# A Flamingo block on one core: rows of the wide expert blocks turned by SBUF-to-SBUF DMAs and VectorE in place of TensorE

## The chip, the cores and the metric

The kernel runs on one core of a Trainium2 chip. The metric is the device time of one execution in microseconds (us), the median of the runs. The engines are TensorE (PE; PEld is its weight load), VectorE (DVE), ScalarE (ACT), GpSimd (POOL) and SyncE (SP), which only issues DMAs here. Each works through its own queue of instructions in program order; semaphores tie them together.

## The reference

The input is x of 4 x 1024 rows of 256 numbers. It computes

```
x = x + tanh(g_xattn) * cross_attention(layernorm(x), ctx)     # 16 heads, 77 context rows
x = x + tanh(g_ffn) * ffn(layernorm(x))
ffn(x) = silu(x sg^T) * (x su^T) sd^T                          # shared expert, 688 wide
       + sum over 4 experts e: comb[e] * (silu(x eg[e]^T) * (x eu[e]^T)) ed[e]^T
```

where comb holds the weights of the two best experts of each row and zero for the others. All is fp32; the kernel splits a matmul operand into a high and a low fp32r part and makes three products (high*high, high*low, low*high).

## The kernel before

The first 450 us hold the attention, the shared expert, the routing table and the preparation of the experts' weights. The 4096 rows are normalised once and stored in DRAM (xn_scratch). After routing, the 8192 pairs of row and expert, sorted by expert, are worked off in 13 wide blocks of 512 rows (NB = 13, BT = 4 tiles of 128 rows) and then 15 narrow tiles of 128 rows (small_tiles). The change is in the wide blocks (big_tiles) and in the first narrow tile.

For wide block j:

- GpSimd gathers the 512 rows with four indirect DMAs (L501) into big_xin, and adds the four result tiles into the output with four more (L509). Its queue runs: gather j+2, additions of block j, gather j+3, and so on. A gather waits until big_xin is free.
- TensorE transposes big_xin in eight 128x128 squares (x_T, L605) into two PSUM banks, p_m and p_t. This is done at chunk 3 of block j-1.
- ScalarE copies them as the high part, big_fxT_hi (x_hi, L522), and VectorE subtracts that from PSUM and writes the low part, big_fxT_lo (x_lo, L554).
- The hidden width of 688 is worked in six chunks (FC = 6, chunk 5 being short). For each chunk c TensorE computes gate and up (gate_up, L623, 12 matmuls of 512 columns), ScalarE takes the silu (L537), VectorE the product (inner, L569), ScalarE its high part (h_hi, L542), VectorE the low part (h_lo, L576 and L579), and TensorE multiplies chunk c-2 by the down weights (down, L640). ScalarE (weights_hi, L529) and VectorE (weights_lo, L562) copy out the expert's weights three chunks ahead.
- At chunk 1 VectorE scales the four result tiles of block j-1 (result, L586) from the two banks p_f.

The order on each engine is written out by hand. At chunk 3 ScalarE runs silu, weights_hi, h_hi, then the two x_hi of block j+1; VectorE runs inner, h_lo, weights_lo, then the two x_lo. Gate/up of chunk 0 of block j+1 waits for both x_lo:

```
            if c == 0:
                pe.wait_ge(s_xlo, rows_done(j))
```

At the seam between the wide blocks and the narrow tiles, VectorE's step of tile 0 multiplies, scales the last four result tiles (last_results), and then makes the low part of tile 1's rows (x_lo in small_tiles, L274), for which TensorE's gate/up of tile 1 (L341) waits. SP has no work in the wide blocks; its last is storing the shared expert's results. Block 0's rows are turned while the preparation of the experts' weights ends: TensorE's last preparation transposes (of raw and tail) come after gate/up of chunk 1 of block 0.

Of the kernel before, what the change touches and what calls it, by code (L numbers as in the profile page):

```python
# [5 lines left out]
f32r = mybir.dt.float32r  # L6
# [6 lines left out]
P = 128  # L13
# [16 lines left out]
E = 4  # L30
# [25 lines left out]
CUT = FF - P // 2  # L56

# [91 lines left out]
def small_tiles(nc, v, sem, place, banks, s_add):  # L149
# [129 lines left out]
    def on_vector(dve, last_results):  # L279
# [159 lines left out]
def big_tiles(nc, v, m, place, banks):  # L439
# [6 lines left out]
    (s_rows, s_xT, s_xhi, s_xlo, s_whi, s_wlo, s_gu, s_sil, s_hid, s_hhi, s_hlo, s_last, s_y, s_yo, s_add,  # L446
     s_turn) = (m[k] for k in (
         "s_rows s_xT s_xhi s_xlo s_whi s_wlo s_gu s_sil s_hid s_hhi s_hlo s_last s_y s_yo s_add s_turn").split())
# [4 lines left out]
    fxT.append([sb(f"big_fxT1_{s}", [P, KC, WIDE], f32r) for s in ("hi", "lo")])  # L453
# [40 lines left out]

    def on_gpsimd(pool):
        def gather(j):
            if j > 0:
                pool.wait_ge(s_xT, rows_done(j - 1))
# [15 lines left out]
    def on_scalar(act):  # L514
# [31 lines left out]
    def on_vector(dve):  # L546
# [4 lines left out]

        def x_lo(j, c):
            dve.wait_ge(s_xhi, rows_done(j, c))
            nc.vector.tensor_tensor(fxT[j % 2][1][:, c, :], p_x[c][:, :], fxT[j % 2][0][:, c, :],  # L554
                                    ALU.subtract).then_inc(s_xlo, 1)
# [35 lines left out]
        return hold, x_lo, weights_lo, inner, h_lo, result  # L591

    def on_tensor(pe):
# [5 lines left out]
        def x_T(j):  # L599
            pe.wait_ge(s_rows, 16 * BT * (j + 1))  # L600
            if j > 0:
                pe.wait_ge(s_xlo, rows_done(j - 1))
# [5 lines left out]
        def gate_up(j, c):  # L608
# [8 lines left out]
            for half in range(2 if c < FC - 1 else 1):  # L617
                for k in range(KC):
                    for q, (w, x) in enumerate(PASSES):
# [3 lines left out]
                        last = nc.tensor.matmul(p_gu[c % 2][half][0:out_rows, :], lhsT, fxT[j % 2][x][:, k, :],  # L623
# [23 lines left out]
        return hold, x_T, gate_up, down  # L647

    return {"gpsimd": on_gpsimd, "scalar": on_scalar, "vector": on_vector, "tensor": on_tensor}


def attend_share_route(nc, v):
# [8 lines left out]
    with st:  # L661
# [159 lines left out]
        s_add, s_rows = sem("s_add"), sem("s_rows")  # L821
# [3 lines left out]
        big = big_tiles(nc, v, {"s_rows": s_rows, "s_xT": s_xnT, "s_xhi": s_xnhi, "s_xlo": s_xnlo, "s_whi": s_whi,  # L825
# [104 lines left out]
        def _(sp):  # L930
# [1020 lines left out]
        def _(dve):  # L1951
# [650 lines left out]
            hold, x_lo, weights_lo, big_inner, big_h_lo, big_result = big["vector"](dve)  # L2602
# [13 lines left out]
            def big_step(j, c):  # L2616
# [26 lines left out]
            def last_results():  # L2643
                for t in range(BT):
                    big_result(NB - 1, t)
# [4 lines left out]
        def _(pe):  # L2650
# [567 lines left out]
            hold, big_x_T, big_gate_up, big_down = big["tensor"](pe)  # L3218
            big_x_T(0)
# [3 lines left out]
            def big_step(j, c):  # L3223
# [65 lines left out]
```

## Time and profile before

| | |
|---|---|
| median of 3 runs | 884.07 us (882.83 to 884.09) |
| the profiled execution | 881.68 us, its span 879.9 us |
| TensorE busy | 846.5 us, 96% |
| VectorE busy | 581.9 us, 66% |
| ScalarE busy | 520.8 us, 59% |
| GpSimd busy | 461.2 us, 52% |
| wide blocks | from about 453 us to about 769 us |
| DMA | 62.05 MB in 56887 packets |

The span goes from the first to the last instruction; busy is the time in which an engine had an instruction under way. TensorE's matmuls are pipelined, so that one starts before the last has ended: its price is the distance between starts, not the duration shown. A share over the whole span says nothing of a stage.

### The profile page before, as it was taken

How to read it: one execution, taken by the hardware profiler on the slowest of the kernel's cores; microseconds unless marked ns; L12 is line 12 of the kernel's file. 1: busy time of each engine (PE TensorE's matmuls, PEld its weight loads, DVE VectorE, ACT ScalarE, POOL GpSimd, SP SyncE). 2: the span in 40 equal slices, each digit the busy share in tenths (PEclk: the TensorE clock that was granted, in tenths of full speed). 3: DMA queues.
4: the chain of work that ended last, by engine and by line, in shares of the span. 5: the costliest groups of instructions: out<-in, count | busy, mean ns of one | idle time of the engine just before them, and what ended most of it. 6: DMA issues, size and time to landing. Idle time of an engine off the chain costs nothing.

```text
span 879.9 us, 19161 instructions
## 1 busy us (share of the span) xinstructions
PE 846.5 (96%) x6271; PEld 742.7 (84%) x6272; DVE 581.9 (66%) x1203; ACT 520.8 (59%) x1846; POOL 461.2 (52%) x551
## 2 busy tenths in 40 slices
PE   8788999999999999999999999999999999999995
PEld 7566788888888799999988888888888888889994
DVE  6899899999998577876564555555555545444442
ACT  4999999999999444656464444444445444322221
POOL 6686767667565353676531454444443444364442
PEclk9899999999999999999999999999999999999998
DMA  7125233322313222333240333222222232232221
GB/s 219 42 77 180 68 90 94 90 66 90 90 66 96 73 74 85 120 103 103 86 141 25 49 49 49 43 41 38 41 41 42 47 48 37 31 49 42 36 40 20
DMA packets 56887, 62.05 MB, mean 71 GB/s; under 512 B 15642, under 2 KB 45183, under 8 KB 56799
## 3 DMA queue, kind: packets, MB, share of 16 engines
q1 hardware_dynamic: 42871, 43.15, 15.8%
q0 software_dynamic: 12864, 17.57, 12.7%
q8 instruction: 48, 0.79, 0.4%
q14 instruction: 40, 0.33, 0.1%
q10 hardware_dynamic: 1064, 0.21, 0.1%
HBM read 34.78 MB, written 25.82 MB: 69 GB/s over the span
## 4 chain that ended last, share of the span: by engine, by line
PE 85%; ACT 5%; DVE 5%; issue 2%; DMA 1%; POOL 1%; DVEq 0%; SPq 0%; ACTq 0%; POOLq 0%
PE p_s L623 23%; PE p_f L640 12%; PE p_f L2767 9%; PE p_s L341 6%; PE p_f L2812 5%; PE p_s L2767 4%; ACT prob L1484 4%; PE p_t L2698 3%; PE p_t L352 3%; PE p_s L2684 3%; PE p_m L2725 3%; PE p_m L2665 2%; PE p_m L2713 2%; PE p_s L2812 2%; PE p_s L2870 1%
## 5 line engine op out<-in xcount | busy, mean ns | idle before, releaser
L509 POOL DMA_INDIRECT out_rows<-big_yout,slot_id x52 | 86.6, 1666 | 158.2 <-DVE big_yout L586 146.3
L1484 ACT ACTIVATE prob<-p_s,negmax 128x77 f32<-128x77 f32 x512 | 161.1, 372 | 7.2 <-DVE negmax L2032 7.0
L537 ACT ACTIVATE big_sil<-p_s 128x512 f32<-128x512 f32 (+1 forms) x78 | 46.6, 597 | 144.7 <-PE p_s L623 126.1
L1484 ACT ACTIVATION_READ_ACCUMULATOR prob<-p_s,negmax 128x1 f32 x512 | 128.9, 255 | 0.0
L569 DVE TENSOR_TENSOR big_hid<-p_s,big_sil 128x512 f32<-128x512 f32 (+1 forms) x78 | 54.0, 692 | 99.5 <-ACT big_sil L537 88.5
L623 PE MATMUL p_s<-big_fxT_hi,big_w_hi 128*128 128x512 f32 (+1 forms) x286 | 113.8, 398 | 0.3 <-ACT big_w_hi L529 0.3
L623 PE MATMUL p_s<-big_fxT_lo,big_w_hi 128*128 128x512 f32 (+1 forms) x286 | 112.7, 394 | 0.0
L623 PE MATMUL p_s<-big_fxT_hi,big_w_lo 128*128 128x512 f32 (+1 forms) x286 | 112.2, 392 | 0.0
L1108 POOL TENSOR_TENSOR prob<-prob,rinv 128x616 f32<-128x616 f32 x64 | 78.5, 1236 | 62.1 <-DVE rinv L2039 62.1
L1127 POOL TENSOR_TENSOR shT_lo<-shid,shT_hi 128x256 fp32r<-128x256 f32 x80 | 63.0, 800 | 44.4 <-ACT shT_hi L1526 44.3
L640 PE MATMUL p_f<-wd_hi,big_hT_hi 128*128 (+1 forms) x312 | 85.5, 280 | 0.0
L640 PE MATMUL p_f<-wd_lo,big_hT_hi 128*128 (+1 forms) x312 | 85.3, 279 | 0.0
L2767 PE MATMUL p_f<-xnT_hi,swgu_hi 128*128 128x256 f32 x248 | 75.5, 304 | 0.8 <-DVE shid L2055 0.8
L640 PE MATMUL p_f<-wd_hi,big_hT_lo 128*128 x260 | 72.7, 279 | 0.0
L2767 PE MATMUL p_f<-xnT_hi,swgu_lo 128*128 128x256 f32 x248 | 69.6, 281 | 0.0
L2767 PE MATMUL p_f<-xnT_lo,swgu_hi 128*128 128x256 f32 x248 | 69.5, 280 | 0.0
L576 DVE TENSOR_TENSOR big_hT_lo<-big_hid,big_hT_hi 128x512 fp32r<-128x512 f32 (+1 forms) x65 | 44.9, 690 | 35.6 <-ACT big_hT_hi L542 28.6
L501 POOL DMA_INDIRECT big_xin<-xn_scratch,slot_id x52 | 51.4, 989 | 31.9 <-issue 17.2
L623 PEld LDWEIGHTS p_s<-big_fxT_hi,big_w_lo 128*128 128x128 f32 (+1 forms) x286 | 53.0, 185 | 13.1
L542 ACT ACTIVATE big_hT_hi<-big_hid 128x512 fp32r<-128x512 f32 (+1 forms) x78 | 49.3, 632 | 23.1 <-DVE big_hid L569 21.4
L623 PEld LDWEIGHTS p_s<-big_fxT_hi,big_w_hi 128*128 128x128 f32 (+1 forms) x286 | 53.0, 185 | 10.3 <-DVE big_fxT_lo L554 0.5
L640 PEld LDWEIGHTS p_f<-wd_hi,big_hT_hi 128*128 128x128 f32 (+1 forms) x312 | 58.6, 188 | 3.5
(341 smaller groups left out, 2537.7 us busy)
## 6 DMA issues: line engine op xcount, KB each, us to landing
xr<-in_x SPq DMA_DIRECT2D x16, 256.0 KB, 2.9
x_scratch<-xr SPq DMA_DIRECT2D x16, 256.0 KB, 2.8
xn_scratch<-xn SPq DMA_DIRECT2D x16, 256.0 KB, 2.1
xt_scratch<-xnT SPq DMA_DIRECT2D x16, 256.0 KB, 3.2
xin<-xt_scratch SPq DMA_DIRECT2D x16, 256.0 KB, 3.6
x1in<-x_scratch SPq DMA_DIRECT2D x16, 256.0 KB, 3.3
out_rows<-syout SPq DMA_DIRECT2D x16, 256.0 KB, 2.2
raw<-in_L_ffn_ed SPq DMA_DIRECT2D x4, 688.0 KB, 4.3
```

The lines of the kernel that those rows point to most:

```text
L341: last = nc.tensor.matmul(p_gu[:, g0:g1], fxT[a][:, c, :], wgu[b][:, bass.ds(e * KC + c, 1), g0:g1], start=(c == 0 and q == 0), stop=(c == ...
L501: pool.indirect_dma_start(xin[:, t, :], None, v["xn_d"], bass.IndirectOffsetOnAxis(slot_id[:, column(j, t)], 0)).then_inc(s_rows, 16)
L509: pool.indirect_dma_start(out, bass.IndirectOffsetOnAxis(slot_id[:, column(j, t)], 0), yout[:, t, :], None, compute_op=ALU.add).then_inc(s ...
L542: act.activation(hT[n % 3][0][0:r, :], hid[n % 2][0:r, :], ACT.Copy).then_inc(s_hhi, 1)
L569: nc.vector.tensor_tensor(hid[n % 2][0:r, :], up, sil[n % 2][0:r, :], ALU.mult).then_inc(s_hid, 1)
L623: last = nc.tensor.matmul(p_gu[c % 2][half][0:out_rows, :], lhsT, fxT[j % 2][x][:, k, :], start=(k == 0 and q == 0), stop=(k == KC - 1 and ...
L640: last = nc.tensor.matmul(p_y[t // 2][:, t % 2 * H:(t % 2 + 1) * H], hT[n % 3][h][0:r, at], wd[w][0:r, bass.ds(e * FC + c, 1), :], start=( ...
L1108: pool.tensor_tensor(pr_, pr_, rinv[:, t, m * HH:(m + 1) * HH].unsqueeze(2).broadcast_to([P, HH, SK]), ALU.mult).then_inc(s_P, 1)
L1127: pool.tensor_tensor(hT[1][:, c, :], hid[:, c, :], hT[0][:, c, :], ALU.subtract).then_inc(s_hlo, 1)
L1484: last = act.activation(prob[n % 2][t][:, m * PW + h * SK:m * PW + (h + 1) * SK], p_s[:, 2 * t + h // 4, col:col + SK], ACT.Exp, bias=negm ...
L2767: last = nc.tensor.matmul(bank[:, j * UT * P:(j + 1) * UT * P], swgu[w][:, k, j * SGU + c * P:j * SGU + (c + 1) * P], xns[x][:, n % 2, k, ...
L2812: nc.tensor.matmul(bank[:, t * H:(t + 1) * H], hT[x][:, c, at], swd[w][:, c, :], start=(c == 0 and q == 0), stop=False)
```

## The change

For blocks 1 to 12 TensorE no longer transposes. When the gathered rows have landed, SP issues 16 DMAs that place the sixteen 32x32 block positions of every 128x128 square transposed as blocks (rows 32b to 32b+31, columns 32a to 32a+31 go to partitions 32a and on, columns 32b and on) in a new tile, big_placed. VectorE then turns each 32x32 block in place (flip, two instructions of 128x512), into big_turned, which lies over the low part's memory. x_hi and x_lo read it instead of PSUM. The flips stand at chunk 3 of the block before, where x_lo stood, and the two x_lo move to chunk 4. SP's placing waits for the rows, for the flip of the block before and, for the first, for the end of the preparation. GpSimd's gathers wait for the placing instead of the transposes. fxT is laid out by tile and then by half, so that gate/up reads it in four runs of 128 columns. Block 0 is still transposed by TensorE.

At the seam the first narrow tile now takes two of the last four results, then x_lo of tile 1, then the other two.

```diff
@@ small_tiles, on_vector, step @@
-            if isinstance(j, int) and j == 0:
-                last_results()
+            first = isinstance(j, int) and j == 0
+            if first:
+                last_results(0)
             if not last:
                 x_lo(j + 1)
+            if first:
+                last_results(1)
@@ big_tiles @@
-    fxT = [[sb(f"big_fxT0_{s}", [P, KC, WIDE], f32r) for s in ("hi", "lo")]]
+    fxT = [[sb(f"big_fxT0_{s}", [P, BT, KC, P], f32r) for s in ("hi", "lo")]]
...
+    placed = sb("big_placed", [P, BT * KC, P])
...
+    def all_placed(j):
+        return 16 * SIDES * SIDES * j
+
+    def on_sync(sp):
+        def place(j):
+            sp.wait_ge(s_rows, 16 * BT * (j + 1))
+            if j > 1:
+                sp.wait_ge(s_flip, 2 * (j - 1))
+            rows = xin[:, :, :].rearrange("p t (k i) -> p (t k) i", k=KC)
+            for a in range(SIDES):
+                for b in range(SIDES):
+                    sp.dma_start(placed[a * TURN:(a + 1) * TURN, :, b * TURN:(b + 1) * TURN],
+                                 rows[b * TURN:(b + 1) * TURN, :, a * TURN:(a + 1) * TURN]).then_inc(s_placed, 16)
...
         def gather(j):
-            if j > 0:
-                pool.wait_ge(s_xT, rows_done(j - 1))
+            if j == 1:
+                pool.wait_ge(s_xT, rows_done(0))
+            elif j > 1:
+                pool.wait_ge(s_placed, all_placed(j - 1))
@@ on_scalar, x_hi, for j > 0 @@
-            act.wait_ge(s_xT, rows_done(j, c))
-            act.activation(fxT[j % 2][0][:, c, :], p_x[c][:, :], ACT.Copy).then_inc(s_xhi, 1)
+                act.wait_ge(s_flip, 2 * (j - 1) + c + 1)
+                act.activation(fxT[j % 2][0][:, pair, :, :].rearrange("p t k i -> p (t k i)"),
+                               turned[j % 2][:, pair, :, :].rearrange("p t k i -> p (t k i)"),
+                               ACT.Copy).then_inc(s_xhi, 1)
@@ on_vector @@
+        def flip(j, c):
+            dve.wait_ge(s_placed, all_placed(j))
+            if j > 1:
+                dve.wait_ge(s_gu, chunks_done(FC * (j - 1)))
+            blocks = slice(2 * KC * c, 2 * KC * (c + 1))
+            pair = slice(2 * c, 2 * c + 2)
+            nc.vector.transpose(turned[j % 2][:, pair, :, :].rearrange("p t k i -> p (t k i)"),
+                                placed[:, blocks, :].rearrange("p n i -> p (n i)")).then_inc(s_flip, 1)
@@ on_tensor, gate_up @@
-  lhsT, fxT[j % 2][x][:, k, :],
+  lhsT, fxT[j % 2][x][:, :, k, :],
@@ the queue of SP, behind the last store_y @@
+            place = big["sync"](sp)
+            sp.wait_ge(s_etr, PER * E)
+            sp.wait_ge(s_tail, 2 * E + 2)
+            for j in range(1, NB):
+                place(j)
@@ the queue of VectorE, big_step @@
-                        x_lo(j + 1, 0)
-                        x_lo(j + 1, 1)
+                        flip(j + 1, 0)
+                        flip(j + 1, 1)
+                if c == 4 and not last:
+                    x_lo(j + 1, 0)
+                    x_lo(j + 1, 1)
@@ the queue of TensorE, big_step @@
-                if c == 3:
-                    if j < NB - 1:
-                        big_x_T(j + 1)
-                    else:
-                        pe.wait_ge(s_xnlo, NU + KC * NB)
-                        small_x_T(0, 0)
+                if c == 3 and j == NB - 1:
+                    pe.wait_ge(s_xnlo, NU + KC * NB)
+                    small_x_T(0, 0)
```

## Rows read from the trace of the kernel before

**Rows 1.** The page: TensorE in 40 slices, in tenths, and its granted clock.

```profile
PE   8788999999999999999999999999999999999995
PEclk9899999999999999999999999999999999999998
```

**Rows 2.** Timeline of TensorE in block 8: start us, us, engine, line, operation, operands.

```profile
660.99 0.60 PE L605 MATMUL p_m<-ident,big_xin 128*128 128x128 f32 x4
...
661.78 0.47 PE L623 MATMUL p_s<-big_fxT_hi,big_w_hi 128*112 128x512 f32 x1
...
668.81 0.40 PE L623 MATMUL p_s<-big_fxT_hi,big_w_hi 128*128 128x512 f32 x1
```

**Rows 3.** Timeline of ScalarE in block 8; in brackets its idle time and releaser.

```profile
659.78 0.60 ACT L537 ACTIVATE big_sil<-p_s 128x512 f32<-128x512 f32 x1 [2.21 <-PE p_s L623]
...
661.14 0.63 ACT L542 ACTIVATE big_hT_hi<-big_hid 128x512 fp32r<-128x512 f32 x1 [0.24 <-DVE big_hid L569]
661.68 0.58 ACT L522 ACTIVATE big_fxT_hi<-p_m 128x512 fp32r<-128x512 f32 x1
...
664.81 0.60 ACT L537 ACTIVATE big_sil<-p_s 112x512 f32<-112x512 f32 x1 [2.07 <-issue]
```

**Rows 4.** Timeline of VectorE in block 8.

```profile
660.41 0.69 DVE L569 TENSOR_TENSOR big_hid<-p_s,big_sil 128x512 f32<-128x512 f32 x1 [1.91 <-ACT big_sil L537]
661.80 0.69 DVE L576 TENSOR_TENSOR big_hT_lo<-big_hid,big_hT_hi 128x512 fp32r<-128x512 f32 x1 [0.70 <-ACT big_hT_hi L542]
662.41 0.42 DVE L562 CAST big_w_lo<-wgu_lo 128x512 fp32r x1
662.75 0.68 DVE L554 TENSOR_TENSOR big_fxT_lo<-p_m,big_fxT_hi 128x512 fp32r<-128x512 f32 x1
...
665.44 0.69 DVE L569 TENSOR_TENSOR big_hid<-p_s,big_sil 112x512 f32<-112x512 f32 x1 [1.41 <-ACT big_sil L537]
666.83 0.69 DVE L576 TENSOR_TENSOR big_hT_lo<-big_hid,big_hT_hi 112x512 fp32r<-112x512 f32 x1 [0.70 <-issue]
667.44 0.48 DVE L562 CAST big_w_lo<-wgu_lo 128x512 fp32r x1
```

**Rows 5.** Timeline of GpSimd from block 8 into block 9.

```profile
654.82 2.00 POOL L509 DMA_INDIRECT out_rows<-big_yout,slot_id  x1 [11.30 <-DVE big_yout L586]
...
662.86 1.01 POOL L501 DMA_INDIRECT big_xin<-xn_scratch,slot_id  x1 [0.44 <-issue]
...
666.72 0.95 POOL L501 DMA_INDIRECT big_xin<-xn_scratch,slot_id  x1 [0.30 <-issue]
678.93 2.00 POOL L509 DMA_INDIRECT out_rows<-big_yout,slot_id  x1 [11.26 <-DVE big_yout L586]
```

**Rows 6.** Timelines of block 0: TensorE, GpSimd and VectorE, a row of each.

```profile
459.72 0.38 PE L2867 MATMUL p_m<-ident,tail 128*128 128x128 f32 x2
...
455.42 0.95 POOL L501 DMA_INDIRECT big_xin<-xn_scratch,slot_id  x1 [0.30 <-issue]
...
470.11 0.68 DVE L554 TENSOR_TENSOR big_fxT_lo<-p_m,big_fxT_hi 128x512 fp32r<-128x512 f32 x1
```

**Rows 7.** SP's copies by line (ns min/median/max), and the page's DMA queue and issue.

```profile
L952 SPq DMA_DIRECT2D vblk<-vall x96: 544/744/1162, 19.0 to 240.9; - x96
...
L146 SPq DMA_DIRECT2D raw<-in_L_ffn_eu x4: 521/523/523, 81.3 to 441.1; - x4
...
q1 hardware_dynamic: 42871, 43.15, 15.8%
...
xn_scratch<-xn SPq DMA_DIRECT2D x16, 256.0 KB, 2.1
```

**Rows 8.** Timelines at the seam: VectorE, then TensorE.

```profile
771.00 1.65 DVE L586 TENSOR_SCALAR big_yout<-p_f,slots 128x256 f32<-128x256 f32 x4
772.57 0.41 DVE L274 TENSOR_TENSOR fxT_lo<-p_m,fxT_hi 128x256 fp32r<-128x256 f32 x1
...
773.14 0.90 PE L341 MATMUL p_s<-wgu_hi,fxT_hi 128*128 x3 [0.78 <-DVE fxT_lo L274]
```

More of the change, by code:

```diff
@@ L56 @@
 CUT = FF - P // 2
+TURN = 32
+SIDES = P // TURN
 PASSES = ((0, 0), (0, 1), (1, 0))
@@ L445, in big_tiles @@
     p_x, p_gu, p_y = banks
-    (s_rows, s_xT, s_xhi, s_xlo, s_whi, s_wlo, s_gu, s_sil, s_hid, s_hhi, s_hlo, s_last, s_y, s_yo, s_add,
-     s_turn) = (m[k] for k in (
-         "s_rows s_xT s_xhi s_xlo s_whi s_wlo s_gu s_sil s_hid s_hhi s_hlo s_last s_y s_yo s_add s_turn").split())
+    (s_rows, s_xT, s_placed, s_flip, s_xhi, s_xlo, s_whi, s_wlo, s_gu, s_sil, s_hid, s_hhi, s_hlo, s_last, s_y, s_yo,
+     s_add, s_turn) = (m[k] for k in (
+         "s_rows s_xT s_placed s_flip s_xhi s_xlo s_whi s_wlo s_gu s_sil s_hid s_hhi s_hlo s_last s_y s_yo s_add "
+         "s_turn").split())
     sb = Home(nc, *place["ring"]).sb
     xin = sb("big_xin", [P, BT, H])
-    fxT = [[sb(f"big_fxT0_{s}", [P, KC, WIDE], f32r) for s in ("hi", "lo")]]
+    fxT = [[sb(f"big_fxT0_{s}", [P, BT, KC, P], f32r) for s in ("hi", "lo")]]
     sb = Home(nc, *place["raw"]).sb
-    fxT.append([sb(f"big_fxT1_{s}", [P, KC, WIDE], f32r) for s in ("hi", "lo")])
+    fxT.append([sb(f"big_fxT1_{s}", [P, BT, KC, P], f32r) for s in ("hi", "lo")])
+    placed = sb("big_placed", [P, BT * KC, P])
+    turned = []
+    for k, home in enumerate(("ring", "raw")):
+        sb = Home(nc, *place[home]).sb
+        if home == "ring":
+            sb("big_xin_again", [P, BT, H])
+        sb(f"big_fxT{k}_hi_again", [P, BT, KC, P], f32r)
+        turned.append(sb(f"big_turned{k}", [P, BT, KC, P]))
     sb = Home(nc, *place["th"]).sb
@@ L520, in x_hi @@
         def x_hi(j, c):
-            act.wait_ge(s_xT, rows_done(j, c))
-            act.activation(fxT[j % 2][0][:, c, :], p_x[c][:, :], ACT.Copy).then_inc(s_xhi, 1)
+            pair = slice(2 * c, 2 * c + 2)
+            if j == 0:
+                act.wait_ge(s_xT, rows_done(j, c))
+                act.activation(fxT[0][0][:, :, c, :], p_x[c][:, :].rearrange("p (t i) -> p t i", t=BT),
+                               ACT.Copy).then_inc(s_xhi, 1)
+            else:
+                act.wait_ge(s_flip, 2 * (j - 1) + c + 1)
+                act.activation(fxT[j % 2][0][:, pair, :, :].rearrange("p t k i -> p (t k i)"),
+                               turned[j % 2][:, pair, :, :].rearrange("p t k i -> p (t k i)"),
+                               ACT.Copy).then_inc(s_xhi, 1)
         def weights_hi(n):
@@ L550, in hold @@
             dve.reg_load(held[j % 2], expert_of[0:1, j:j + 1])
+        def flip(j, c):
[3 more added lines that the diff above has]
+            blocks = slice(2 * KC * c, 2 * KC * (c + 1))
+            pair = slice(2 * c, 2 * c + 2)
+            nc.vector.transpose(turned[j % 2][:, pair, :, :].rearrange("p t k i -> p (t k i)"),
+                                placed[:, blocks, :].rearrange("p n i -> p (n i)")).then_inc(s_flip, 1)
         def x_lo(j, c):
             dve.wait_ge(s_xhi, rows_done(j, c))
-            nc.vector.tensor_tensor(fxT[j % 2][1][:, c, :], p_x[c][:, :], fxT[j % 2][0][:, c, :],
-                                    ALU.subtract).then_inc(s_xlo, 1)
+            if j == 0:
+                nc.vector.tensor_tensor(fxT[0][1][:, :, c, :], p_x[c][:, :].rearrange("p (t i) -> p t i", t=BT),
+                                        fxT[0][0][:, :, c, :], ALU.subtract).then_inc(s_xlo, 1)
+            else:
+                low, whole, high = (x[:, 2 * c:2 * c + 2, :, :].rearrange("p t k i -> p (t k i)")
+                                    for x in (fxT[j % 2][1], turned[j % 2], fxT[j % 2][0]))
+                nc.vector.tensor_tensor(low, whole, high, ALU.subtract).then_inc(s_xlo, 1)
         def weights_lo(n):
@@ L589, in result @@
                 last.then_inc(s_yo, 1)
-        return hold, x_lo, weights_lo, inner, h_lo, result
+        return hold, flip, x_lo, weights_lo, inner, h_lo, result
     def on_tensor(pe):
@@ L597, in hold, with first_x_T @@
             pe.reg_load(held[j % 2], expert_of[0:1, j:j + 1])
[L599 to L602, printed above, removed]
+        def first_x_T():
+            pe.wait_ge(s_rows, 16 * BT)
             for c in range(KC):
@@ L622, in gate_up @@
                         out_rows = r if c < FC - 1 else 2 * r
-                        last = nc.tensor.matmul(p_gu[c % 2][half][0:out_rows, :], lhsT, fxT[j % 2][x][:, k, :],
+                        last = nc.tensor.matmul(p_gu[c % 2][half][0:out_rows, :], lhsT, fxT[j % 2][x][:, :, k, :],
                                                 start=(k == 0 and q == 0), stop=(k == KC - 1 and q == 2))
@@ L645, in down @@
                     last.then_inc(s_y, 1)
-        return hold, x_T, gate_up, down
-    return {"gpsimd": on_gpsimd, "scalar": on_scalar, "vector": on_vector, "tensor": on_tensor}
+        return hold, first_x_T, gate_up, down
+    return {"sync": on_sync, "gpsimd": on_gpsimd, "scalar": on_scalar, "vector": on_vector, "tensor": on_tensor}
 def attend_share_route(nc, v):
@@ L820, in attend_share_route @@
             "s_spread", "s_row", "s_til", "s_val", "s_vid", "s_vlo", "s_table"))
-        s_add, s_rows = sem("s_add"), sem("s_rows")
+        s_add, s_rows, s_placed, s_flip = (sem(n) for n in ("s_add", "s_rows", "s_placed", "s_flip"))
         late = small_tiles(nc, v, sem, {"ring": ring, "x1in": (x1in_home, xns_home), "raw": (raw_home, tail_home),
@@ L2601, in _ @@
                 e_lo(G)
-            hold, x_lo, weights_lo, big_inner, big_h_lo, big_result = big["vector"](dve)
+            hold, flip, x_lo, weights_lo, big_inner, big_h_lo, big_result = big["vector"](dve)
             hold(0)
@@ L2641, in _, with last_results @@
                     big_step(j, c)
-            def last_results():
-                for t in range(BT):
-                    big_result(NB - 1, t)
+            def last_results(pair):
+                for t in range(2):
+                    big_result(NB - 1, 2 * pair + t)
             late["vector"](dve, last_results)
```

7 lines of the change are left out of this document (4 added, 3 removed).

## The prediction

> **What bounds the kernel now.** I read the page first, for the slices: over the thirteen wide blocks TensorE's slices stand at 9 and its granted clock too, and neither falls until the last slice [rows 1]. So in the blocks TensorE sets the pace, and time taken off it is gained as long as nothing else is late. To see what would be late next I read the timelines of one block (block 8) engine by engine. TensorE runs gate/up of chunk 3, a share of the down product, then eight transposes of the next block's rows (the row shows the first four) from 660.99 to 661.78, then gate/up of chunk 4, and it enters block 9 at 668.81 without a pause [rows 2]. ScalarE and VectorE idle between short bursts and seem to have room [rows 3, 4]; but each is a queue in program order, and inside a chunk they alternate (silu, product, high part, low part), so what counts is the length of that chain and not their busy share. GpSimd's queue shows the period: the first addition of results is issued at 654.82 and again at 678.93, so a block takes 24.11 us [rows 5].
>
> **What is removed.** Eight transposes per block, 0.79 us of TensorE by the difference of starts (661.78 - 660.99) [rows 2]. Twelve of the thirteen blocks lose them: 12 x 0.79 = 9.5 us, if TensorE stays the bound. The page "TensorE: Matmul & The Clock Gate" of the Trainium skill (Part 4) gives about 275 ns for such a transpose in a kernel, so eight would be 2.2 us and twelve blocks 26 us by it; the trace's starts, about 0.1 us apart, are against that reading, and I keep 0.79.
>
> **What is added on the chain.** This is the step that decides. Before, x_hi and x_lo of the next block read PSUM as soon as TensorE had transposed, and the two subtracts were over about 1.3 us after 662.75, before the silu of chunk 4 at 664.81 [rows 3, 4]. Now at chunk 3 VectorE does flip, flip in the place of x_lo, x_lo; ScalarE's two x_hi wait for the flips, and ScalarE's silu of chunk 4 stands behind them; VectorE's x_lo, x_lo come only after the low part and the weights of chunk 4, and the next block's first gate/up waits for the second. I lay that chain out on block 8's clock, with F the duration of a flip and f the distance to the start of the next instruction:
> Silu of chunk 3 starts at 659.78, the first flip where the first x_lo stood, at 662.75 [rows 3, 4]. The second flip starts at 662.75 + f and ends at 662.75 + f + F. The second x_hi starts 0.04 later, as the high part does behind the product (660.41 + 0.69, then 661.14). It reads SBUF now, so I give it the high part's distance to the next start, 0.54 (661.68 - 661.14): silu of chunk 4 starts at 663.33 + f + F. From silu to product is 0.63 (665.44 - 664.81), to the low part 1.39 (666.83 - 665.44), to the weights 0.61 (667.44 - 666.83), to the first x_lo 0.34 (662.75 - 662.41), to the second x_lo 0.61 (a subtract that reads two SBUF tiles, as 661.80 to 662.41), its duration 0.69, and 0.16 until TensorE's matmul starts, as at the seam (772.57 + 0.41, then 773.14) [rows 3, 4, 8]. Sum: 4.43 us, so block 9 starts at 667.76 + f + F, where it started at 668.81 before. TensorE alone would be there at 668.81 - 0.79 = 668.02. Hence the rule of this change: the pace is unchanged at f + F = 1.05; each us more costs 1 us a block; the full 9.5 us come only if f + F is below 0.26.
>
> **The price of a flip.** The trace has no VectorE transpose. Each flip is 128x512 fp32. Bounds: below, the cast of the same size at 0.42 with 0.34 to the next start [rows 4]: f + F = 0.76. It reads two elements a cycle, which the other rows do not: 128x256 takes 0.41 and 128x512 takes 0.68 on a subtract from PSUM [rows 4, 8], 1.05 ns an element. Above, twice that time per element: 512 x 2 x 1.05 ns + 0.15 = 1.23, 1.15 to the next start, f + F = 2.38. I take one element a cycle with the fixed part of an SBUF instruction, the subtract's 0.69 and 0.61 [rows 4]: f + F = 1.30. Block 9 then starts at 669.06, 0.25 late; TensorE idles about 1.0 us ahead of each block instead of transposing for 0.8. Twelve blocks: **+3.0 us**. The page "VectorE: DVE Perf Modes" (The three transpose paths) speaks against the change: VectorE turns only 32x32 blocks and takes 311 ns for a 128x128 square. Four squares in a flip would be 1.24 us by it, which is the upper bound; whether 512 columns pay the page's fixed part four times no run here shows.
>
> **Placing the rows.** Sixteen DMAs a block leave SP, each 32 partitions by 8 runs of 128 bytes, 4096 runs a block. SP has nothing else then. Issue: the SBUF-to-SBUF copies of before took 0.54 to 1.16 us each (median 0.74), a 48-row copy 0.52 [rows 7]; I take the latter, nearest in being a multiple of 16 rows, plus 0.04 between two: 16 x 0.56 = 9.0 us, and 2.1 us for the last to land [rows 7]: D = 11 us. Bounds of D: 2.1 below, if issuing costs nothing; 16 x 1.20 + 2.1 = 21.3 above. The transfers themselves are small: queue 1 moved 42871 packets in 15.8% of 16 engines' 880 us, 0.052 us each [rows 7]; 4096 at that price on 16 engines are 13 us, and these packets are an eighth as long. Room: the gather of block j+2 waits for the additions before it and for the placing; its four issues start at 662.86, the last ends at 667.7 [rows 5], about 2 us to land, so placing runs from 669.8, and the flips want it 24.1 after 662.75, at 686.9. D may be 17.1 us. Free in the steady state, by 6 us.
> Block 0 has less room: place(1) waits for the last preparation transposes of TensorE, over at 460.1, and the flips are due at 470.11; its rows were gathered by about 458.4 [rows 6]. 460.2 + 11 = 471.2: **+1.1 us**, once; bounds 0 and 11.4, by those of D. The gathers' new wait is behind additions that are done; behind it in GpSimd's queue stand the next block's additions, due at 678.93, 11 us after the last gather [rows 5].
>
> **The seam.** At the first narrow tile x_lo moves ahead of two of the four results. TensorE waited 0.78 us there for it [rows 8]. It would start after two results, at 771.00 + 2 x 0.41 = 771.82, not 772.57: **-0.75 us**; its x_hi must be done by then, which the rows neither show nor exclude. The two results behind it take 0.8 us and end at about 773.0, where they used to end at 772.7, so nothing new is late. Bounds -0.8 and 0. The strided order of fxT (runs of 128) I cost at nothing; no row shows another price, and its bounds are 0 and the 1.0 us of idle in each block that covers it.
>
> **Sum.** 3.0 + 1.1 - 0.75 = +3.4 us on the profiled execution's 881.68 (span 879.9 and 1.8 around it). That execution is 2.4 us under the median of the runs, 884.07; the change is put on the median: 884.07 + 3.4 = **887.5 us**. A difference under 0.2% (1.8 us) this measurement cannot tell from none.
>
> **Rivals.**
> A, the forecast: one element a cycle; f + F between 1.2 and 1.45 and handoffs as in the rows give +0.15 to +0.4 a block, with block 0 from 0 to +3: 885.5 to 892. Chance 0.48.
> B, slow flips: two cycles an element or a fixed part per square, f + F = 2.38: 2.38 - 1.05 = +1.33 a block, +16, with the rest 900.4. For it: no row shows a VectorE transpose, and it is a different data path. Against: all other fp32 rows lie at one element a cycle or better. Chance 0.14.
> C, placing becomes the bound: D above 17.1. With SP at 1.16 us an issue, D = 21.3 and a block is 6.9 (gather and landing) + 21.3 = 28.2, +4.1 each: 12 x 4.1, 11.4 in block 0 and -0.75 give about +60, 944. For it: small SBUF copies are the dearest issues of SP. Against: the median copy gives D = 16 x 0.78 + 2.1 = 14.6, still free. Chance 0.06.
> D, the other side: flips run at the cast's rate, f + F = 0.76: -0.29 a block, -3.5; with block 0 and the seam -3.1: 881.0. The point where it decides is f + F = 1.05 less what block 0 costs. Also a shorter handoff than in the rows would lead here. Chance 0.16.
> E, within 0.2%: f + F about 1.1, or the seam and a punctual block 0 offset the blocks. Chance 0.16.
>
> **How the numbers follow.** Slower: A, B and C, 0.68; same 0.16; faster 0.16. C is left out above and the lower part of D below: the range runs from 881 to 901, the likeliest case's own from 885.5 to 892.
>
> **What would show it.** Right: no transposes on big_xin after block 0; TensorE idle about 1 us ahead of the first gate/up of each block, released by VectorE's big_fxT_lo; silu of chunk 4 released by x_hi or starting 0.7 us after gate/up ended; flips about 0.69 us; a period of 24.3 to 24.4; SP's placing done several us before its flips, except in block 0. Wrong: TensorE without that idle time (the chain is shorter than laid out, period 23.3), flips near 0.4 or 1.2 us, or VectorE's flips released by a DMA in each block. A granted clock that falls because of the idle us in each block would make all of it worse.

## The result and the profile after

The changed kernel takes 889.62 us (median of 4 runs, 888.60 to 890.69) and the kernel before 883.45 us (4 runs); the ratio is 1.0071, its 95% interval 1.0055 to 1.0087, or +4.9 to +7.7 us. It is slower, as forecast (887.5, range 881 to 901). Timed once more on another occasion it took 891.08 us beside 882.94, ratio 1.0087 (1.0074 to 1.0101). The forecast was a difference of +3.4 us; measured are +6.2 and +8.1. The profiled execution is the slowest of the first four, 890.69 us, span 889.0.

Who waited for whom on TensorE in the changed kernel, from 440 us on: us in total, times, longest.

```profile
PE p_s L675 <- DVE big_fxT_lo L609: 12.2, 12, 2.7
PE p_t L391 <- DVE hT_hi L317: 0.8, 1, 0.8
PE p_m L331 <- DMA xin<-xn_scratch,get_at: 0.7, 1, 0.7
```

The first line is the forecast's mark: TensorE waits for x_lo once per block, twelve times; 2.7 us of it are block 0's, 9.4 the other eleven's. The second is no effect of the change: the kernel before has it too (L386, 0.8 us). The last line was not forecast. VectorE, ScalarE and TensorE in block 8 of the changed kernel, the rows that answer to [rows 2 to 4]:

```profile
669.56 0.42 DVE L616 CAST big_w_lo<-wgu_lo 128x512 fp32r x1
669.90 1.30 DVE L598 STREAM_TRANSPOSE big_turned<-big_placed 128x512 f32<-128x512 f32 x2
672.38 0.69 DVE L623 TENSOR_TENSOR big_hid<-p_s,big_sil 112x512 f32<-112x512 f32 x1 [1.18 <-ACT big_sil L577]
...
674.39 0.55 DVE L616 CAST big_w_lo<-wgu_lo 128x512 fp32r x1
674.86 1.27 DVE L609 TENSOR_TENSOR big_fxT_lo<-big_turned,big_fxT_hi 128x512 fp32r<-128x512 f32 x2
```

```profile
666.93 0.60 ACT L577 ACTIVATE big_sil<-p_s 128x512 f32<-128x512 f32 x1 [2.21 <-PE p_s L675]
...
670.64 1.23 ACT L560 ACTIVATE big_fxT_hi<-big_turned 128x512 fp32r<-128x512 f32 x2 [1.72 <-DVE big_turned L598]
671.77 0.58 ACT L577 ACTIVATE big_sil<-p_s 112x512 f32<-112x512 f32 x1
```

```profile
676.19 0.50 PE L675 MATMUL p_s<-big_fxT_hi,big_w_hi 128*128 128x512 f32 x1 [0.90 <-DVE big_fxT_lo L609]
```

The two flips take 1.30 us together, 0.69 each, with 0.61 from one start to the next. From silu of chunk 3 to silu of chunk 4 it is 671.77 - 666.93 = 4.84 us; the prediction's chain has 663.33 + 1.30 - 659.78 = 4.85. The silu of chunk 4 has no idle time in front of it: it ran right behind x_hi, and not when TensorE was ready. From silu of chunk 3 to the next block's first matmul it is 9.26 us (676.19 - 666.93), by the chain 9.28, before 9.03. In the block before this one it is 9.13 us.

GpSimd's first additions of two blocks show the period, and SP's placing:

```profile
661.97 2.00 POOL L541 DMA_INDIRECT out_rows<-big_yout,slot_id  x1 [9.52 <-DVE big_yout L640]
...
686.37 2.00 POOL L541 DMA_INDIRECT out_rows<-big_yout,slot_id  x1 [11.69 <-DVE big_yout L640]
```

```profile
L520 SPq DMA_DIRECT2D big_placed<-big_xin x192: 585/611/1418, 461.8 to 735.0; - x192
```

24.40 us here and 24.26 to 24.33 in every other block. Over the eleven periods between the first additions of blocks 0 to 11 the mean is 24.33 us. The kernel before alternates too, between 24.11 [rows 5] and 24.05, with a mean of 24.07. So a block takes 0.26 us more. All mean periods below are taken in this way. A copy is issued in 0.61 us. In block 0 (timelines of VectorE and TensorE) the first placing is late:

```profile
473.74 1.30 DVE L598 STREAM_TRANSPOSE big_turned<-big_placed 128x512 f32<-128x512 f32 x2 [1.85 <-DMA big_placed<-big_xin]
```

```profile
479.90 0.50 PE L675 MATMUL p_s<-big_fxT_hi,big_w_hi 128*128 128x512 f32 x1 [2.72 <-DVE big_fxT_lo L609]
```

SP issued from 461.83, its last issue ended at 472.41, and the flips could start at 473.74: 11.9 us, where the prediction had 11. And the clock, from the view by stretches (busy us of PE, PEld, DVE, ACT, POOL, each with its count, then the granted clock, DMA share, GB/s):

```profile
477.00:480.00 3.00, 0.28 (x3) 0.10 (x1) 2.35 (x5) 1.58 (x3) 2.69 (x2) 1.00 0.29 87
480.00:481.00 1.00, 1.00 (x4) 0.80 (x5) 0.57 (x1) 0.40 (x1) 0.66 (x1) 0.90 0.00 0
481.00:484.00 3.00, 3.00 (x8) 2.31 (x7) 1.11 (x2) 0.23 (x1) 0.00 (x0) 0.50 0.22 55
```

Shortly after TensorE had stood still for 2.72 us, its granted clock fell to half (1.2 GHz in place of 2.4) for about 3.4 us, and 8 matmuls ran in three us where 13 would at the distance of 0.23 us that they have at the full clock.

### The profile page after: what moved, and what is told of

Its sections match the earlier page's. It is cut to its first block, busy times and chain, and to the rows that moved or that the text cites. A ratio compares the mean times of both kernels' runs of the same rounds, so it can differ in the third digit from the quotient of the medians.

```text
span 889.0 us, 19207 instructions
## 1 busy us (share of the span) xinstructions
PE 842.8 (95%) x6175; PEld 734.7 (83%) x6176; DVE 596.8 (67%) x1227; ACT 522.6 (59%) x1846; POOL 470.5 (53%) x551
## 4 chain that ended last, share of the span: by engine, by line
PE 70%; DVE 10%; ACT 9%; issue 5%; DMA 2%; SPq 1%; POOL 1%; DVEq 0%; ACTq 0%; POOLq 0%
PE p_s L675 17%; PE p_f L2827 9%; PE p_f L692 6%; PE p_s L346 6%; PE p_f L2872 4%; PE p_s L2827 4%; ACT prob L1541 3%; PE p_t L2758 3%; PE p_s L2744 3%; PE p_t L357 3%; PE p_m L2773 2%; PE p_m L2725 2%; PE p_m L2785 2%; PE p_s L2872 2%; DVE big_fxT_lo L609 2%
## 5 line engine op out<-in xcount | busy, mean ns | idle before, releaser
L533 POOL DMA_INDIRECT big_xin<-xn_scratch,slot_id x52 | 60.7, 1167 | 33.8 <-DMA big_placed<-big_xin 16.4
```

The lines of the kernel that those rows point to most:

```text
L533: pool.indirect_dma_start(xin[:, t, :], None, v["xn_d"], bass.IndirectOffsetOnAxis(slot_id[:, column(j, t)], 0)).then_inc(s_rows, 16)
```

## The experiments

A sum that several of them use is the stretch from the start of the first to the start of the last gate/up matmul of the wide blocks, by the profiles (us):

```
before 309.92   changed 316.47, again 316.68   old seam 315.01   block 1 by TensorE 313.14
x_lo late alone 315.20   x_hi late 309.03   flips early 300.58   flips early, block 1 by TensorE 300.51
idle transposes 316.85   flips by squares 321.38
```

Each run was timed beside the kernel before, which had medians of 882.94 us (the first four) and 882.81 us (the others).

The mean periods of a block tell how the cost is made up: 24.07 us before, 24.51 with x_lo late alone, 24.33 changed, 23.64 with x_hi late, 23.21 with the flips early. Taking the transposes away is worth 0.86 us (24.07 - 23.21), x_lo's later place costs 0.44 (24.51 - 24.07; 23.64 - 23.21 gives 0.43, though flips and x_hi are moved there too), and the two x_hi, waiting for the flips in front of the silu, cost 0.69 (24.33 - 23.64). Together: 24.07 - 0.86 + 0.43 + 0.69 = 24.33.

**The changed kernel again.** No edit.

> The changed kernel once more, for its difference to the kernel before and for the granted clock. Its first profile had two stretches of 3.4 us at half clock that the profile of before has not: at 40.5 us, in the attention, which the change does not touch, and at 480.8 us, right behind the 2.7 us pause of TensorE at the end of block 0. Theory of the chain (the flips push ScalarE's silu of chunk 4 and with it the low parts of the next block): 12 x 0.29 us, 1.8 us more in block 0 and, if the clock falls there again, 1.7 us; 5.2 to 7 us over before, 888.5 to 890.5. Rival, the clock: the stretches come and go from run to run; then a profile without them should lie 3.4 us lower, and the rest be 5.3.

Measured 891.08 us, +8.1. TensorE's pauses are 12.3 us in twelve, the longest 2.7, and the clock fell again behind that one (at 482.5 us). The short fall in the attention was there too. For the wide blocks it repeats the first profile; the rival is taken up below.

**x_hi late.** ScalarE's queue alone:

```diff
-                    else:
-                        x_hi(j + 1, 0)
-                        x_hi(j + 1, 1)
+                if c == 4 and not last:
+                    x_hi(j + 1, 0)
+                    x_hi(j + 1, 1)
```

> The changed kernel with one edit: ScalarE's two x_hi stand at the end of chunk 4 and not of chunk 3, so the silu of chunk 4 no longer stands behind them and the flips. Theory of the chain: silu of chunk 4 starts when TensorE is ready (4.15 us after that of chunk 3, not 4.84), the low part and the weights end 0.7 us earlier, the x_hi then follow the high part of chunk 4 and x_lo follows them; the next block starts about 0.35 us after TensorE could. Period 23.7 in place of 24.40, twelve times 0.7: 8 us under the changed kernel, about 881.5. Rival (the flips and x_lo are too much for VectorE, or placing is late): no change, 889.5.

Measured 879.60 us, ratio 0.9959 (0.9945 to 0.9972): 10 to 11.5 us under the changed kernel, and under the kernel before. The period is 23.68 us (657.14 to 680.82, the starts of two blocks' first additions), as expected. The silu now comes 4.19 us behind that of chunk 3 (662.10), released by TensorE and ahead of x_hi:

```profile
666.29 0.60 ACT L577 ACTIVATE big_sil<-p_s 112x512 f32<-112x512 f32 x1 [2.20 <-PE p_s L675]
...
668.18 1.14 ACT L560 ACTIVATE big_fxT_hi<-big_turned 128x512 fp32r<-128x512 f32 x2
```

By the periods it gains 11 x 0.69 = 7.6 us; the rest of the 10 to 11.5 is not explained. Its profiled execution is its slowest, 883.62 us. Flips, placing and x_lo are what they were; two copies in another place in ScalarE's queue decide between a loss and a gain.

**Flips early.** VectorE's queue alone; x_lo returns to the end of chunk 3:

```diff
                 big_inner(n)
+                if c == 3 and not last:
+                    flip(j + 1, 0)
+                    flip(j + 1, 1)
...
-                        flip(j + 1, 0)
-                        flip(j + 1, 1)
-                if c == 4 and not last:
-                    x_lo(j + 1, 0)
-                    x_lo(j + 1, 1)
+                        x_lo(j + 1, 0)
+                        x_lo(j + 1, 1)
```

> The changed kernel with VectorE's order changed: the two flips right behind the product of chunk 3, the two x_lo back at the end of chunk 3 where they were before the change. Theory of the chain: the second flip ends at 662.3 on block 8's clock of before, the second x_hi at 662.95, before silu of chunk 4 is due at 663.94, the second x_lo at 664.5; nothing is late and the period is TensorE's own, 23.3. Against the changed kernel 11 x 1.1 = 12 us less in the steady blocks, but block 0's placing is now due 1.7 us earlier and costs about as much as before: 877 to 879. Rival (placing is late in every block, since the flips want it 1.7 us earlier): TensorE's pauses stay and VectorE's flips are released by the DMA; 885 or more.

Measured 874.84 us, ratio 0.9905 (0.9890 to 0.9920). VectorE in chunk 3 of one block:

```profile
657.44 0.69 DVE L623 TENSOR_TENSOR big_hid<-p_s,big_sil 128x512 f32<-128x512 f32 x1 [1.92 <-ACT big_sil L577]
658.05 1.29 DVE L598 STREAM_TRANSPOSE big_turned<-big_placed 128x512 f32<-128x512 f32 x2
659.26 0.65 DVE L630 TENSOR_TENSOR big_hT_lo<-big_hid,big_hT_hi 128x512 fp32r<-128x512 f32 x1
659.84 0.42 DVE L616 CAST big_w_lo<-wgu_lo 128x512 fp32r x1
660.17 1.28 DVE L609 TENSOR_TENSOR big_fxT_lo<-big_turned,big_fxT_hi 128x512 fp32r<-128x512 f32 x2
661.63 0.69 DVE L623 TENSOR_TENSOR big_hid<-p_s,big_sil 112x512 f32<-112x512 f32 x1 [0.17 <-issue]
```

The flips fill the 0.7 us in which VectorE used to wait for the high part [rows 4], and everything is over 0.17 us before the next product. TensorE's only pause left in the wide blocks is 0.5 us, of block 0 (apart from 0.3 us at their very start, which the kernel before has too). The blocks take 300.58 us, 9.3 less than before. Better than expected (877 to 879), because block 0's late placing costs almost nothing in this order and because the transposes were worth more than 0.79 us a block: behind them TensorE's first gate/up matmul took 0.32 us to the next start (661.78 to 662.10) and not 0.23, so they cost 0.88, and the period says 0.86.

**Flips early, block 1 by TensorE.** The same, and the placing starts with block 2 (its counts and waits shifted by one block):

```diff
+                if c == 3 and j == 0:
+                    first_x_T(1)
...
-            for j in range(1, NB):
+            for j in range(2, NB):
                 place(j)
```

> As the one with early flips, and block 1 too is transposed by TensorE, so that the first placing has all of block 1's time. Theory of the chain: no pause of TensorE at all in the wide blocks, and no fall of its clock behind it; 11 blocks lose 0.79 us, 8.7 us under the kernel before, less what later waits of the narrow tiles take back: 875 to 876. Rival (the room of the placing is too small at a period of 23.3: gather and landing 6.9, sixteen copies 11.9, together 18.8): pauses of TensorE that grow from block to block, 878 or more.

Measured 874.37 us, ratio 0.9903 (0.9888 to 0.9918), the same as the last within the error. The period is 23.24 us (651.34 to 674.58) and no matmul of the wide blocks waits for a row. So placing has enough room at this period too, though gather, landing and copies fill 18.8 us of it.

**Old seam.** The changed kernel with last_results(0), last_results(1) and then x_lo.

> The changed kernel with the seam as before: all four last results, then x_lo of tile 1. The prediction put the new seam at -0.75 us. The profile of the changed kernel shows TensorE going through the seam without the 0.78 us pause, but 12 us later it waits 0.7 us for the gathered rows of narrow tile 3, which it did not before. Theory: the seam's gain is given back at that gather, which GpSimd's own queue times; so no difference to the changed kernel (0 to 0.1 us), and in this profile 0.8 us of pause at the seam and none at the gather. Rival, as predicted: 0.75 us slower than the changed kernel. In the profile the stretch from the last gate/up of the wide blocks to the end decides: 107.0 before, 107.3 and 107.5 with the change.

Measured 889.56 us (changed: 889.62 and 891.08); its executions lie between 889.0 and 893.1, so the medians alone could not tell 0.75 us from none. The profiles can. From the last gate/up of the wide blocks to TensorE's last matmul it is 107.1 us, with the new seam 107.3 and 107.5, before 107.0; to the end of the span 118.0, with the new seam 117.8 and 117.9, before 117.0: no gain. The order changes which line shows a wait; first this kernel, then the changed one:

```profile
PE p_s L345 <- DVE fxT_lo L276: 0.8, 1, 0.8
```

```profile
791.99 0.44 PE L331 MATMUL p_m<-ident,xin 128*128 128x128 f32 x2 [0.68 <-DMA xin<-xn_scratch,get_at]
```

This profile also has the 2.7 us pause behind block 0 and no fall of the clock:

```profile
477.00:480.00 3.00, 0.35 (x2) 0.31 (x3) 2.61 (x5) 1.33 (x3) 2.70 (x2) 1.00 0.30 87
480.00:484.00 4.00, 4.00 (x25) 3.55 (x24) 2.10 (x4) 1.75 (x3) 0.41 (x1) 1.00 0.17 41
```

Its blocks take 315.01 us, 1.5 and 1.7 less than in the changed kernel's two profiles. That is the price of the fall. The idle transposes' profile (below) has the 2.7 us pause and no fall as well, and less 11 x 0.17 for its longer period its blocks take 315.0 too.

**Seam alone.** The kernel before with the new seam.

> The kernel before with the new seam alone. Theory: no difference (within 0.1 us), the pause moves from the seam to the gather of tile 3. Rival, as predicted: -0.75 us, 882.2. It also shows whether the short fall of the granted clock at 40 us, in the attention, which the profiles of all five kernels with the placing have and the one of before has not, comes with a kernel that has no placing.

Measured 882.82 us beside 882.81, ratio 0.9999 (0.9990 to 1.0009). The interval, -0.9 to +0.8 us, just reaches the -0.75 of the prediction; the profile decides again: 107.0 us to TensorE's last matmul, as before, and 117.1 to the end beside 117.0. The pause at the seam is gone and this one is there:

```profile
PE p_m L329 <- DMA xin<-xn_scratch,get_at: 0.6, 1, 0.6
```

In this profile, that of the kernel before, the changed one and that with the old seam, GpSimd issues the gather of tile 3 18.0 us behind the last gate/up of the wide blocks, whatever the seam. And this kernel, without any placing, has the short fall of the clock in the attention, while the last one, with the placing, has not. In this order, 36 to 46 us:

```profile
36.00:46.00 10.00, 7.86 (x68) 4.73 (x67) 6.77 (x16) 9.46 (x54) 5.80 (x8) 0.83 0.32 85
```

```profile
36.00:46.00 10.00, 7.62 (x76) 5.18 (x74) 7.94 (x18) 9.45 (x54) 5.74 (x8) 1.00 0.33 85
```

So the fall in the attention is none of the change's effects, though the changed kernel's first profile has it and the one of before has not.

**x_lo late alone.** The kernel before, with x_lo moved:

```diff
-                    else:
-                        x_lo(j + 1, 0)
-                        x_lo(j + 1, 1)
+                if c == 4 and not last:
+                    x_lo(j + 1, 0)
+                    x_lo(j + 1, 1)
```

> The kernel before with one edit: the two x_lo at the end of chunk 4, as the change has them; TensorE still transposes, nothing is placed or flipped. Theory of the chain: x_hi is early and silu of chunk 4 on time at 664.81 on block 8's clock, the weights of chunk 4 are issued at 667.44, x_lo follow at about 667.8 and 668.4 and end at 669.1, TensorE's first gate/up starts at 669.25 and not at 668.81: 0.35 to 0.45 us a block, twelve times: +4 to +5.5, 887 to 888.5. So the later place of x_lo alone would cost more than the whole change does in a steady block, and the transposes' 0.79 us pays a part back. Rival (the flips are what costs, the place of x_lo is free): 883.

Measured 887.47 us, ratio 1.0049 (1.0036 to 1.0062), +4.7. The blocks take 5.3 us more, 0.44 each:

```profile
PE p_s L623 <- DVE big_fxT_lo L554: 1.9, 10, 0.2
```

The blocks lose more than the sum of these waits: 0.2 us of idle time is a loss of 0.44, since a matmul shown as 0.28 long lets the next start after 0.12, and the first gate/up behind a pause takes 0.09 more to the next start. One shift in the old kernel's order, with neither flips nor copies, costs more in a steady block than the whole change (0.44 against 0.26), which has the transposes' time to set against it.

**Idle transposes.** The changed kernel with eight unread transposes of the identity a block, in blocks 1 to 11:

```diff
+                if c == 3 and 0 < j < NB - 1:
+                    for bank in (p_m, p_t):
+                        for t in range(BT):
+                            nc.tensor.transpose(bank[:, t * P:(t + 1) * P], ident[:, :], ident[:, :])
```

> The changed kernel, with eight 128x128 transposes of the identity added to TensorE in each of blocks 1 to 11, where the rows' transposes stood; nobody reads them. Theory of the chain: TensorE pauses 0.87 us a block in any case, so 0.79 us of transposes fit in, the pause falls to 0.1 us and the time stays at 889.5 to 891. So the work that the change takes off TensorE is worth nothing as the change stands. Rival (TensorE is still the bound and its pauses come from a loss elsewhere): 11 x 0.79 = 8.7 us slower, 899.

Measured 891.29 us, against 889.62 and 891.08 of the changed kernel. The period is 24.48 us (662.78 to 687.26). TensorE's pauses behind block 0, for this kernel and then the changed one:

```profile
PE p_s L675 <- DVE big_fxT_lo L609: 1.1, 6, 0.2
```

```profile
PE p_s L675 <- DVE big_fxT_lo L609: 9.4, 11, 0.9
```

8.3 us of pauses became transposes, and the mean period grew by 0.17, from 24.33 to 24.50, not by 0.79. In the changed kernel the work taken off TensorE is worth about a fifth of its time.

**Flips by squares.** Eight flips of 128x128 in place of two of 128x512:

```diff
-            nc.vector.transpose(turned[j % 2][:, pair, :, :]...,
-                                placed[:, blocks, :]...).then_inc(s_flip, 1)
+            for t in (2 * c, 2 * c + 1):
+                for k in range(KC):
+                    one = nc.vector.transpose(turned[j % 2][:, t, k, :], placed[:, KC * t + k, :])
+            one.then_inc(s_flip, 1)
```

> The changed kernel with each flip of 128x512 cut into four of 128x128: eight VectorE transposes a block for the same elements. A subtract of 128x128 takes 0.28 us with 0.2 to the next start; if a transpose pays like it, eight take 7 x 0.20 + 0.28 = 1.68 in place of 1.30. Theory of the chain: each us on the flips costs a us a block: +0.38, twelve times, 4.6 us over the changed kernel, 895. If a square takes the 311 ns of the Trainium skill's page with nothing overlapped, 2.49 - 1.30 = +1.19 a block, 14 us, 904. Rival (the flips are off the path, the pause comes from the place of x_lo alone): no change, 890.

Measured 893.90 us. Each takes 0.27 us and the eight 1.66:

```profile
L600 DVE STREAM_TRANSPOSE big_turned<-big_placed x96: 265/269/311, 474.8 to 748.7; 128x128 f32<-128x128 f32 x96
...
673.48 1.66 DVE L600 STREAM_TRANSPOSE big_turned<-big_placed 128x128 f32<-128x128 f32 x8
```

+0.36 us on the flips made the period 24.64 us (640.91 to 665.55), 24.62 on the mean, +0.29. Against the changed kernel's shorter blocks it is 24.64 - 24.26 = +0.38, as expected; its longer ones hold a slower cast of the weights, which is never slow here (last section). The rival of a block unchanged by the flips is out. Of the 4.9 us that the wide blocks take over the changed kernel's, 1.7 are block 0's, where TensorE's pause was 4.4 us in this profile: SP's issues took 10.6 us as before, but the last copy landed 2.7 us behind them and not 1.3.

**Halved copies.** 32 copies of half the length:

```diff
+                    for half in (slice(0, BT), slice(BT, 2 * BT)):
...
-        return 16 * SIDES * SIDES * j
+        return 2 * 16 * SIDES * SIDES * j
```

> The changed kernel with each placing DMA cut in two halves (four runs of 128 bytes a partition and not eight): 32 copies a block, the same bytes. The issue took 0.61 us each with 0.04 between; if it does not depend on the runs, placing takes 32 x 0.65 + 1.5 = 22.3 us, over the room of 17.1 worked out in the prediction. Gather and landing 6.9, so a block takes about 29.2 in place of 24.4: twelve times 4.8 less what block 0 has, plus 10.4 us more in block 0: about +60 over the changed kernel, 950. If the issue goes with the runs (0.3 us each), nothing changes, 890. Rival (the room is larger than worked out, since gathers could run ahead): +10 alone, from block 0.

Measured 981.69 us, ratio 1.1112 (1.1096 to 1.1128). The issue does not depend on the runs:

```profile
L521 SPq DMA_DIRECT2D big_placed<-big_xin x384: 585/601/2145, 462.5 to 831.1; - x192
```

```profile
610.40 1.30 DVE L600 STREAM_TRANSPOSE big_turned<-big_placed 128x512 f32<-128x512 f32 x2 [5.66 <-DMA big_placed<-big_xin]
641.59 1.30 DVE L600 STREAM_TRANSPOSE big_turned<-big_placed 128x512 f32<-128x512 f32 x2 [4.25 <-DMA big_placed<-big_xin]
```

```profile
600.00:631.20 31.20, 24.69 (x129) 21.14 (x128) 13.46 (x26) 10.59 (x19) 10.73 (x8) 0.84 0.31 50
```

The period is 31.2 us here and 31.6 on the mean (30.8 to 33.2), set by gather, landing and copies: the prediction's case C is real, and twice the copies bring it about. It is 2 us more than the 29.2 worked out, and in this block little of that is the copies: GpSimd's gathers start 0.8 us after the flips could (611.20), their rows have landed 7.9 us later (619.10) where 6.9 was expected, since the last gather's issue takes 2.27 us in place of 0.95, the 32 issues end at 640.33, and the flips start 1.3 us after that. In the longest blocks single copies took up to 2.1 us. Behind TensorE's pauses of 5 to 7 us its clock is at half for a part of each block (mean 0.84 here). The flips wait for the copies in every steady block, so the copies set the pace; that the clock costs nothing beside them is argued and not shown.

**Late flips, block 1 by TensorE.** The changed kernel with the edit of two experiments above, but flips and x_lo where the change has them.

> The changed kernel with one edit: block 1 too is transposed by TensorE; flips and x_lo stay where the change puts them. It takes out the late first placing of block 0 and TensorE's 2.7 us pause there, behind which three of five profiles with it show the granted clock at half for 3.4 us. Theory: block 0 then costs its transposes and a late x_lo (+0.4) in place of +1.9 and, with the fall, 1.7: 1.5 to 3.2 us under the changed kernel, 886.5 to 888.5; no fall of the clock behind block 0, and eleven pauses of 0.87. Rival (the fall has nothing to do with the pause): a half-clock stretch inside the wide blocks all the same.

Measured 887.03 us, ratio 1.0052 (1.0040 to 1.0064), 2.6 to 4 us under the changed kernel. The granted clock does not fall in the wide blocks. Of all profiles, the six whose longest pause there is 0.9 us or less (this one, the kernel before, seam alone, x_lo late, both with early flips) have no fall there; of four with 2.7 us in block 0 two have one, and those with 2.9 us (x_hi late), 4.4 us (by squares) and 13.6 us (halved copies) have one too. As two of four with the 2.7 us pause have no fall, this one profile alone would prove little; the six together do more.

## Why the prediction came out as it did

**The chain: right, with its size.** That TensorE would stop setting the pace, where it would wait, and through which queues, came out as laid out: 9.26 us against 9.28 in block 8. That it is this close is partly luck. The cast of the weights was slow in this block and put 0.47 us and not 0.34 in front of x_lo (674.39 to 674.86), which the last handoff gave back, 0.06 us and not 0.16 (676.13 to 676.19), with 0.03 of the two x_lo; in the block before, with the usual cast, it is 9.13. Forecast +0.25 us a block and +3.0 in all; measured +0.26 on the mean period. By the stretches, the blocks with late flips but without the first placing take 313.14 - 309.92 = 3.2 us more, block 0's own late x_lo included. x_hi late, idle transposes and flips by squares change the chain by one link each and move the mean period by -0.69, +0.17 and +0.29. The strided order of fxT cost nothing, as assumed: the median distance between gate/up matmuls is 0.231 us before and after. The transposes were put 0.09 us too low (0.79, measured 0.86 to 0.88), which does not enter the sum, since the chain and not TensorE sets the time.

**The price of a flip: right.** 0.69 each, the subtract's price, f + F = 1.30. Case B is out, and with it the upper bound of 1.24 us for four squares in a flip: a square of 128x128 fp32 took 0.27 us, with 0.2 to the next start in a row.

**The steady placing: right.** D, the time from SP's first issue until the last copy has landed, was about 11.9 us and the room 17.1. It is issue that costs (0.61 us, not the 0.52 taken), and the placing is never late in a steady block.

**Block 0: mis-sized.** +1.1 forecast; 315.01 - 313.14 = 1.9 measured. The term that was off is D: the sixteen issues took 10.6 us and not 9.0, and the last copy landed 1.3 us behind them and not 2.1. SP's start was as forecast: 461.83, in a profile whose wide blocks begin 1.68 us later than in that of before, answers to 460.15, forecast 460.2.

**The seam: this step failed.** "-0.75 us" was the removed pause, and the pause did go: 0.78 us before, none after. But 12 us later TensorE waits 0.6 to 0.7 us for the rows of tile 3, gathered by GpSimd, whose queue the seam does not move. The prediction asked what the two displaced results would delay and not what TensorE, arriving earlier, would find. By the profiles' stretches behind the wide blocks both experiments on the seam say zero, give or take 0.2 us.

**The clock: named and not priced.** "A granted clock that falls because of the idle us in each block" did not happen for pauses of 0.9 us; behind block 0's 2.7 us it happened in two of four profiles, at 1.5 to 1.7 us each. What decides whether it falls is open.

The sum by the profiles: 3.2 + 1.9 + 0 = 5.1 us without a fall of the clock, 6.6 with it; forecast 3.4, measured 6.2 and 8.1 on the medians. So the forecast time, 887.5 us, was 2.1 and 3.6 us too low, and the steady blocks have no part in it. Nor is the profiled pair's difference all the change's: the spans differ by 9.1 us, of which 6.5 lie in the wide blocks, 1.7 ahead of them and 0.8 behind them. Ahead of them the profiles vary by 2.9 us, and not by kernel (the first gate/up at 452.97 before, at 455.64 with the seam alone, at 454.38 with the old seam). What is over 6.6 in the second timing is open. The mean granted clock of its executions does not order them: 892.21 us at 0.991, 888.56 at 0.990. The executions of the changed kernel spread over 3.6 us in it, those of before over 0.8, but over 3.1 in a later timing. The likeliest case's range, 885.5 to 892, was also added up loosely: with the seam's -0.75 its terms give 885.1 to 891.1.

## What to carry to other kernels

Before taking work off the busiest engine, lay out the chain of short instructions on the others that would have to deliver in its place, in the order of their queues, and compare its end to the second; engines half idle on average can lack the room in the one place that counts. When a change of this kind loses, try the order first: here the same flips and copies give +6 to +8 us in one order of the queues, -3.3 us with two copies later in ScalarE's, and -8.1 us (874.84 against 882.94) with another order of VectorE's. And a pause removed near the end of a stage is gained only if what the engine does next is not timed by another queue.

## What the runs showed of the hardware

- VectorE's 32x32 transposes of fp32 cost what a subtract or product of the same size costs: 0.69 us for 128x512 (0.69), 0.27 for 128x128 (0.28).
- An SBUF-to-SBUF copy of 32 partitions costs SP 0.61 us to issue, with eight runs of 128 bytes a partition as with four (0.60).
- Why the period alternates between 24.40 and 24.26: VectorE's cast of the weights took 0.55 us in one block and 0.42 in the next. The long ones come while GpSimd issues a gather; GpSimd, in the changed kernel (block 8, then block 7):

```profile
673.74 0.94 POOL L533 DMA_INDIRECT big_xin<-xn_scratch,slot_id  x1 [0.30 <-issue]
```

```profile
649.52 2.94 POOL L533 DMA_INDIRECT big_xin<-xn_scratch,slot_id  x1 [0.30 <-issue]
650.02 0.42 DVE L616 CAST big_w_lo<-wgu_lo 128x512 fp32r x1
```

In block 7 the cast takes 0.42 and the gather's issue, which began before it, 2.94 instead of 0.95: one of the two is held up. But the cast is over at 650.44 and the gather's issue at 652.46, so the cast alone is not what holds it. The same is seen in all 44 gathers of over 2 us in the wide blocks of eight profiles (the changed kernel's two, old seam, idle transposes, x_hi late, halved copies, flips by squares, late flips with block 1 by TensorE): each ends 0.09 to 0.10 us after the product of chunk 5 of that block, the last of a row of VectorE's instructions with hardly a pause between them. The page "SBUF — State Buffer" of the Trainium skill (Who interferes with whom) says that a cast can contend with GpSimd for a shared pair of ports, and that whoever issues first has it for the whole instruction while the other fully blocks. The rows agree in that one of the two is held up; they do not show that it is always the later one, since in block 7 the cast, which began 0.5 us after the gather, is not slowed. No run here separates the ports from another cause.
